# Cross-attention and FP4 feed-forward layer: attention added to x by accumulating transfers, low products of h split, block maximum of x taken a step ahead

## The chip, the cores and the metric

One core of one Trainium2 chip runs the kernel. The metric is the device time of one execution, in microseconds; the medians are over several runs. The core has four compute engines that run their own instruction streams: TensorE (PE, with weight loads shown as PEld), VectorE (DVE), ScalarE (ACT) and GpSimd (POOL). SyncE (SP) issues most of the transfers. Streams meet only at semaphores.

## What is computed

`x` is 64 x 128 x 256, the context has the same shape. The layer is

```python
q, k, v = LN(x) @ Wq + bq, ctx @ Wq + bq, ctx @ Wq + bq      # 16 wide
corr = mean over batch and channel of the circular correlation of q and k (by FFT)
w, shift = top 12 of corr, w = softmax(w)
R = sum of w * roll(v, -shift)                               # along the sequence
x = x + broadcast of R over 16 heads, reshaped @ Wout + bout
h = silu(fq(LN(x)) @ fq(w_gate).T) * (fq(LN(x)) @ fq(w_up).T)   # 704 wide
x = x + fq(h) @ fq(w_down).T
```

`fq` quantizes blocks of 16 to the FP4 grid (0, 0.5, 1, 1.5, 2, 3, 4, 6) by the scale max|block| / 6 and multiplies back. Because the heads are a broadcast reshaped along the sequence, the attention of one batch row has only 8 different rows of 256, each used by 16 positions.

## The kernel before

**Prologue (to some 122 us).** The 64 tiles of x (128 positions by 256) are loaded into `xs` and stay there. TensorE transposes x and context and projects them, the correlation is summed in one bank, the FFN weights are quantized and turned, the top 12 are found. At its end the attention (`a_sb`, 4 tiles of 128 x 257, the 257th column being minus the mean of the row) goes to `a_scratch` in DRAM from ACT's queue, one transfer for each quarter of the batch (semaphores `a_io0` to `a_io3`). `neg_mean` holds minus the mean of each row of x.

**Main loop.** 32 pairs of tiles, software-pipelined: every engine runs `for st in range(FIRST, END)`, -5 to 35, each stage working on another pair. The order of work on an engine is the order in which the code is written; an instruction behind a waiting one waits too. A pair goes through these stages:

- SP loads its attention rows (`load_attn`, L332, two transfers of 128.5 KB, each row of the scratch read by 16 partitions) two pairs ahead of their use. GpSimd adds them to `xs` (L453) and to the negative mean (L454).
- ACT squares x minus the mean with a running sum (L548, step n-3). GpSimd makes the reciprocal deviation (L428, L430, L432), ACT normalizes into `xn` (L540, one step later).
- DVE takes the maximum of each block of x (L934, `bm`), one step later the scale (L943, over h's blocks of the pair before and x's together), its reciprocal (L946) and the product `y_x` (L965). ACT's `split` (L467, L468, L470) makes an anchor and a rounded copy, DVE's `offset` (L740) and `grid` (L744) land on the FP4 grid, and L920 multiplies with the high and the low half of the scale (`sh` from ACT L557, `sl` from GpSimd L438 and L444) into fp16 `xq`. SP transposes it (L344).
- TensorE makes gate and up (L704 to L706), ACT silu (L525), DVE the product `hb` (`gate_up`, L915).
- h goes the same way: maximum L930, scale L943, product `y_h` L950, split on ACT, offset, grid, high product L920 on DVE; but its two low products are GpSimd's (`low_h`, L415, one for each tile), both at the start of a step. SP transposes both tiles (`turn_h`, L339), TensorE makes the down projection and adds x through a scaled identity (`down`, L714 to L717), ACT evacuates (`residual`, L530), SP stores (L348).

DVE's order in a step of the full loop is: gate_up of the odd tile, maximum of h, maximum of x, scale, reciprocal, y_h, x offset, x grid, two x products, y_x, gate_up of the even tile, h offset, h grid, h high product. ACT's: residual of the even tile, normalize, squares, sh, silu, residual of the odd tile, split of h, silu, split of x. GpSimd's: two low products, reciprocal deviation, L438, sl, the addition. SP's: store, two transposes of h, transpose of x, store, attention loads.

`h_c` is one buffer, so ACT's split of a pair waits until the low products of the pair before are done (`need(act, s["loh"], 2 * j)`). `xn` is one buffer too.

Of the kernel before, what the change touches and what calls it, by code (L numbers as in the profile page):

```python
# [16 lines left out]
P = 128  # L17
# [46 lines left out]
FIRST, END = -5, NP + 4  # L64
# [16 lines left out]
def build(nc, x, ctx, wq, bq, wout, bout, w_gate, w_up, w_down, out):  # L81
    es = ExitStack()
    with es:  # L83
# [66 lines left out]
        neg_mean = sb("neg_mean", [P, B])  # L150

        s_nm = sb("s_nm", [P, 2, 2])
# [5 lines left out]
        s32 = sb("s32", [P, NS])  # L158
# [5 lines left out]
        h_c = sb("h_c", [P, 2 * FF], U16)  # L164
# [4 lines left out]
        attn = w_raw[:, 2 * FF:2 * FF + 4 * DA].rearrange("p (a t n) -> p a t n", a=2, t=2)  # L169
        xn = w_raw[:, 2 * FF + 4 * DA:2 * FF + 4 * DA + 2 * D]  # L170
# [3 lines left out]
        sq_out = w_raw[:, 2 * FF + 4 * DA + 4 * D:2 * FF + 4 * DA + 6 * D].rearrange("p (t n) -> p t n", t=2)  # L174
        ctx16 = ctx_sb[:, :, :, :].rearrange("p a t d -> p (a t d)").bitcast(F16)
# [12 lines left out]
        def bank16(k):  # L188
# [4 lines left out]
            "c_loaded0", "c_loaded1", "c_loaded2", "c_loaded3", "attn_loaded0", "attn_loaded1",  # L193
# [3 lines left out]
            "x1_done", "sq_done", "pool_st", "xn_ready", "x_max", "sc_steps", "sh_done", "s32", "sl", "x_split", "x4_steps",  # L197
# [8 lines left out]
        attn_loaded = [s["attn_loaded0"], s["attn_loaded1"]]  # L206
# [10 lines left out]
        def runs_of(w, g):  # L217
            o, n = SEGS[g]
            r = RUN_H if n == FF else RUN_X
            return w[:, FF * (g % 2):FF * (g % 2) + n].rearrange("p (ih c r) -> p c ih r", ih=IH, r=r)  # L220

# [47 lines left out]
        def _(sp):  # L269
            def load_x(i):  # L270
                if i >= AHEAD:
                    sp.wait_ge(s["stats"], 2 * (i - AHEAD + 1))
                sp.dma_start(xs[:, QT * i:QT * (i + 1), :], x[QT * i:QT * (i + 1)].rearrange("b l d -> l b d")
                             ).then_inc(x_loaded[i % AHEAD], 16)
# [51 lines left out]
            def load_attn(n):  # L326
                need(sp, s["x1_done"], n - 1)
                if n % (NP // 4) == 0:
                    sp.wait_ge(a_io[n // (NP // 4)], 16)
                for t in range(2):  # L330
                    row = (2 * n + t) * ROWS8 * DA
                    sp.dma_start(attn[:, n % 2, t, :], bass.AP(a_dram.tensor, row, [[0, HEADS], [DA, ROWS8], [1, DA]])  # L332
                                 ).then_inc(attn_loaded[n % 2], 16)

# [15 lines left out]
            load_attn(0)  # L350
            load_attn(1)
# [17 lines left out]
        def _(pool):  # L369
# [18 lines left out]
            def rstd_a(i):  # L388
# [3 lines left out]
                nm = neg_mean[:, QT * i:QT * (i + 1)]  # L392
# [16 lines left out]
            def low_h(j):  # L409
                pool.wait_ge(s["h4_steps"], K_HQ * (j + 1))  # L410
                pool.wait_ge(s["sl"], j + 1 - SC0 + 1)
                for t in range(2):
                    need(pool, hT[2 * (j % 2) + t], 16 * (j // 2))
                for t in range(2):
                    pool.tensor_tensor(  # L415
                        hq[:, j % 2, t, FF:2 * FF].rearrange("p (ih r) -> p ih r", ih=IH),
                        h_c[:, :].bitcast(F16).rearrange("p (ih t r) -> p t ih r", ih=IH, t=2)[:, t],
                        sl[:, (j + 1) % 2, t * RUN_H:(t + 1) * RUN_H].unsqueeze(1).broadcast_to([P, IH, RUN_H]),
                        ALU.mult).then_inc(s["loh"], 1)

            for st in range(FIRST, END):
# [580 lines left out]
```

## Time and profile before

| what | value |
|---|---|
| median of 3 runs | 578.78 us (577.47 to 581.57) |
| profiled execution | 579.47 us, span of its instructions 577.6 us |
| busy share of the span | PE 82%, DVE 80%, ACT 68%, POOL 49% |
| granted TensorE clock, mean | 0.947 |
| main loop, 168 to 543 us | PE 345.2, DVE 345.8, ACT 290.2, POOL 218.1 us busy of 375 |

Busy time counts an instruction from its start to its end, its waits for a port included. A row of the timeline has start, duration, engine, line, operation, output and input with their shapes, and in brackets the idle time before it with what ended it. Starts of neighbouring DVE or ACT instructions can lie closer together than one of them lasts, as they overlap in the engine's pipeline; so distances are taken from start to start.

### The profile page before, as it was taken

To read this page: it belongs to the slowest core of one execution; us is meant where nothing else is said; L and a number is where in the kernel's file an instruction comes from. 1 tells how busy PE (TensorE), PEld (TensorE's weight loads), DVE (VectorE), ACT (ScalarE), POOL (GpSimd) and SP (SyncE) were. 2 spreads that over 40 slices of the span, in tenths; PEclk is the share of its full clock that TensorE was granted. 3 is DMA by queue.
4 is the path that set the end of the run, shared out by engine and by line. 5 is a ranking of instruction groups with operands and counts; after the bars stand their busy time and mean duration, and the time that the engine had idled before them with its cause. 6 is when DMAs were issued, how large, how long until landed. Compare 5 with 4: busy or idle time off the path is not lost. (4 is left out here: it accounts for less than half of the span.)

```text
span 577.6 us, 10039 instructions
## 1 busy us (share of the span) xinstructions
PE 472.7 (82%) x3454; PEld 310.6 (54%) x3454; DVE 460.9 (80%) x742; ACT 393.9 (68%) x666; POOL 281.9 (49%) x365
## 2 busy tenths in 40 slices
PE   5866677631978999999998999999989999999964
PEld 4756566420445555655555556555655556556643
DVE  3588874415698999999989999999999999998660
ACT  4425856716578887777888887878888777777530
POOL 3312353026355566666565566665655666632222
PEclk9996898875989999999999999999999999999978
DMA  8995420033145554655555556664655546544533
GB/s 283 341 350 166 146 64 2 27 92 74 37 87 123 116 119 110 124 127 115 106 120 123 119 115 116 128 124 104 113 126 124 112 108 107 109 96 90 94 77 77
DMA packets 165043, 69.19 MB, mean 120 GB/s; under 512 B 129153, under 2 KB 164737, under 8 KB 164993
## 3 DMA queue, kind: packets, MB, share of 16 engines
q1 hardware_dynamic: 164416, 68.03, 51.8%
q8 instruction: 27, 0.44, 0.3%
q10 hardware_dynamic: 576, 0.53, 0.3%
q14 instruction: 24, 0.19, 0.1%
HBM read 27.90 MB, written 9.18 MB: 64 GB/s over the span
## 5 line engine op out<-in xcount | busy, mean ns | idle before, releaser
L704 PE MATMUL ps<-guT_hi,a_xT 128*128 128x512 f16 (+1 forms) x384 | 140.4, 366 | 55.0 <-DMA a_xT<-ctx_sb 55.0
L415 POOL TENSOR_TENSOR ctx_sb<-h_c,sl 128x704 f16<-128x704 f16 x64 | 96.1, 1522 | 115.8 <-DVE ctx_sb L920 115.8
L714 PE MATMUL ps<-dT_hi,hqT 128*128 128x256 f16 x704 | 133.3, 278 | 10.7 <-DMA hqT<-ctx_sb 10.7
L705 PE MATMUL ps<-guT_lo,a_xT 128*128 128x512 f16 (+1 forms) x384 | 140.2, 365 | 0.0
L706 PE MATMUL ps<-guT_hi,a_xT 128*128 128x512 f16 (+1 forms) x384 | 140.2, 365 | 0.0
L704 PEld LDWEIGHTS ps<-guT_hi,a_xT 128*128 128x128 f16 x384 | 37.8, 98 | 103.6 <-DMA a_xT<-ctx_sb 46.0
L467 ACT ACTIVATE h_c<-y_h 128x1408 bf16<-128x1408 bf16 (+3 forms) x40 | 49.2, 1230 | 61.3 <-DVE y_h L950 36.5
L716 PE MATMUL ps<-dT_lo,hqT 128*128 128x256 f16 x384 | 90.2, 278 | 0.0
L714 PEld LDWEIGHTS ps<-dT_hi,hqT 128*128 128x128 f16 x704 | 70.1, 100 | 23.9 <-DMA hqT<-ctx_sb 11.5
L453 POOL TENSOR_TENSOR xs<-xs,w_raw 128x512 f32<-128x512 f32 x32 | 37.8, 1182 | 75.5 <-issue 49.6
L915 DVE SCALAR_TENSOR_TENSOR hb<-ps,h_in,w_raw 128x704 f32<-128x704 f32 x64 | 60.5, 945 | 4.5 <-PE ps L706 4.4
L706 PEld LDWEIGHTS ps<-guT_hi,a_xT 128*128 128x128 f16 x384 | 37.8, 98 | 39.3 <-issue 1.4
L705 PEld LDWEIGHTS ps<-guT_lo,a_xT 128*128 128x128 f16 x384 | 37.8, 99 | 38.9 <-issue 1.6
L525 ACT ACTIVATE w_raw<-ps,inv_gu 128x704 f32<-128x704 f32 x64 | 53.0, 829 | 6.0 <-PE ps L706 6.0
L740 DVE TENSOR_TENSOR h_t<-h_c,h_t 128x1408 f16<-128x1408 bf16 (+3 forms) x40 | 32.3, 808 | 27.7 <-ACT h_c L470 27.7
L557 ACT ACTIVATE sh<-bm 128x240 bf16<-128x240 f32 (+2 forms) x35 | 13.5, 385 | 59.5 <-DVE bm L943 59.5
L950 DVE TENSOR_TENSOR y_h<-hb,bm 128x1408 f32<-128x1408 f32 x32 | 52.5, 1639 | 1.1
L930 DVE TENSOR_REDUCE bm<-hb 128x88 f32<-128x1408 f32 x32 | 51.8, 1620 | 1.1
L470 ACT ACTIVATE h_c<-h_c,root 128x1408 bf16<-128x1408 bf16 (+3 forms) x40 | 52.2, 1306 | 0.0
L438 POOL TENSOR_SCALAR s<-bm 128x120 f32<-128x120 f32 (+2 forms) x35 | 48.0, 1371 | 3.7 <-DVE bm L943 1.1
L468 ACT ACTIVATE h_t<-y_h 128x1408 f16<-128x1408 bf16 (+3 forms) x40 | 48.5, 1214 | 0.0
L716 PEld LDWEIGHTS ps<-dT_lo,hqT 128*128 128x128 f16 x384 | 38.3, 100 | 8.6 <-issue 0.3
(139 smaller groups left out, 858.5 us busy)
## 6 DMA issues: line engine op xcount, KB each, us to landing
w_raw<-a_scratch SPq DMA_DIRECT2D x64, 128.5 KB, 2.6
xs<-in_x_dram SPq DMA_DIRECT2D x16, 512.0 KB, 8.7
ctx_sb<-in_ctx_dram SPq DMA_DIRECT2D x16, 512.0 KB, 7.8
out_dram<-a_xT SPq DMA_DIRECT2D x64, 128.0 KB, 2.0
hqT<-ctx_sb SPq DMA_TRANSPOSE x64, 3.7
w_raw<-in_L_ffn_w_down_dram SPq DMA_DIRECT2D x1, 704.0 KB, 9.1
w_raw<-in_L_ffn_w_gate_dram SPq DMA_DIRECT2D x1, 640.0 KB, 8.2
w_raw<-in_L_ffn_w_up_dram SPq DMA_DIRECT2D x1, 640.0 KB, 8.4
```

Source lines behind the costliest of these rows:

```text
L415: pool.tensor_tensor(hq[:, j % 2, t, FF:2 * FF].rearrange("p (ih r) -> p ih r", ih=IH), h_c[:, :].bitcast(F16).rearrange("p (ih t r) -> p ...
L467: act.activation(c.bitcast(BF16), top, ACT.Square, scale=ANCHOR_SLOPE).then_inc(done, 1)
L470: act.activation(c.bitcast(BF16), c.bitcast(BF16), ACT.Square, bias=root[:, 0:1]).then_inc(done, 1)
L525: act.activation(sil[:, i % 2, :], gu_out(i)[:, 0:FF], ACT.Silu, scale=inv_gu[:, 0:1]).then_inc(s["sil_done"], 1)
L704: pe.matmul(dst, xt[:, c, :], guT[0][:, c, n0:n1], start=(c == 0), stop=False)
L705: pe.matmul(dst, xt[:, c, :], guT[1][:, c, n0:n1], start=False, stop=False)
L706: last = pe.matmul(dst, xt[:, KC + c, :], guT[0][:, c, n0:n1], start=False, stop=(c == KC - 1))
L714: pe.matmul(dst, hqT[:, j % 4, c, :], dT_hi[:, c, :], start=(c == 0), stop=False)
L716: pe.matmul(dst, hqT[:, j % 4, c, :], dT_lo[:, c, :], start=False, stop=False)
L915: dve.scalar_tensor_tensor(out=h_v, in0=gu_out(i)[:, FF:2 * FF].rearrange(split, ih=IH), scalar=h_in[:, 0:1], in1=sil[:, i % 2, :].rearran ...
L930: dve.tensor_reduce(bm[:, 0, 0:RUN_H], hb[:, :].rearrange("p (ih b il) -> p b ih il", ih=IH, il=2), AX.XY, ALU.max, apply_absolute_value=T ...
L950: dve.tensor_tensor(y_h[:, :].rearrange(runs, ih=IH, il=2), hb[:, :].rearrange(runs, ih=IH, il=2), bm[:, 2, 0:RUN_H].unsqueeze(1).unsqueez ...
```

## The change

1. `load_attn`, `attn`, `neg_mean`, `s_nm` and the additions L453 and L454 go. `xs` gets a 257th column that holds minus the mean (written in place by GpSimd in the prologue; ACT reads it as bias). The scratch is laid out as 8 rows of all batches, and 13 transfers on GpSimd's own queue add it to `xs` while they move (`accum_op`), for 1, 2, 2, 3, then three times 3, 3, 2 pairs. The first two are issued ahead of the loop, then two in each step until all are out, each time behind the reciprocal deviation. `xs` is then loaded with rows of 1024 B at a distance of 1028 B.
2. The low products of h are issued apart: the first at the start of the step, the second at the end of GpSimd's step, behind a wait for `y_x` of the same step. `h_c` gets a second buffer; SP transposes the odd tile of h behind x.
3. The maximum of x is taken a step earlier, behind y_x and ahead of gate_up of the even tile. Normalize, reciprocal deviation and squares move a step ahead with it; `xn` gets a second buffer, and the loop starts at -4 in place of -5.
4. L438 (`s32`) goes: the factors X_SCALE and DOWN move into the constants, `bm[:, 1]` is read directly by sh and sl, and so the next scale on DVE waits for `sl` in place of `s32`.

```diff
-FIRST, END = -5, NP + 4
+FIRST, END = -4, NP + 4
+SUMS = (1, 2, 2, 3) + 3 * (3, 3, 2)
-        a_dram = nc.dram_tensor("a_scratch", [B * ROWS8, DA], F32, kind="Internal").ap()
-        xs = sb("xs", [P, B, D])
+        a_dram = nc.dram_tensor("a_scratch", [ROWS8, B * DA], F32, kind="Internal").ap()
+        xs = sb("xs", [P, B, DA])
...
-        xn = w_raw[:, 2 * FF + 4 * DA:2 * FF + 4 * DA + 2 * D]
+        xn = w_q[0][:, :].bitcast(F32)[:, 0:4 * D].rearrange("p (a n) -> p a n", a=2)
+        h_c = [h_c0[:, :], w_q[1][:, 0:2 * FF].bitcast(U16)]
...
 SP:
                 if pair_ok(st - 2):
                     turn_h(2 * st - 4)
-                    turn_h(2 * st - 3)
                 if pair_ok(st + 1):
                     turn_x(st + 1)
+                if pair_ok(st - 2):
+                    turn_h(2 * st - 3)
...
-                if pair_ok(st + 6) and st + 6 >= 2:
-                    load_attn(st + 6)
 GpSimd:
+            def add_attn(k):
+                n0 = sum(SUMS[:k])
+                if n0 % (NP // 4) == 0:
+                    pool.wait_ge(a_io[n0 // (NP // 4)], 16)
+                row, cols = 2 * n0 * DA, 2 * SUMS[k] * DA
+                pool.dma_start(xs[:, 2 * n0:2 * (n0 + SUMS[k]), :].rearrange("p t n -> p (t n)"),
+                               bass.AP(a_dram.tensor, row, [[0, HEADS], [B * DA, ROWS8], [1, cols]]), accum_op=ALU.add
+                               ).then_inc(s[f"x1_in{k}"], 16)
...
+            pool.wait_ge(s["trx"], 2 * NQ)
+            for k in range(2):
+                add_attn(k)
             for st in range(FIRST, END):
                 if pair_ok(st - 2):
-                    low_h(st - 2)
-                n = st + 3
+                    low_h(st - 2, 0)
+                n = st + 4
...
+                for k in (2 * (st - FIRST) + 2, 2 * (st - FIRST) + 3):
+                    if k < len(SUMS):
+                        add_attn(k)
                 if scaled(st):
...
-                    pool.tensor_scalar(s32[:, n0:n1], bm[:, 1, n0:n1], X_SCALE * DOWN, 1.0, ALU.mult, ALU.mult).then_inc(s["s32"], 1)
-                    pool.wait_ge(s["s32"], m + 1)
...
-                n = st + 4
-                if pair_ok(n):
...
-                    x1 = xs[:, 2 * n:2 * n + 2, :]
-                    pool.tensor_tensor(x1, x1, attn[:, n % 2, :, 0:D], ALU.add)
...
+                if pair_ok(st - 2):
+                    if pair_ok(st + 2):
+                        pool.wait_ge(s["x4_steps"], K_XQ * (st + 2) + 1)
+                    low_h(st - 2, 1)
 ACT:
-                j, n, b = st - 1, st + 2, st + 3
+                j, n, e, b = st - 1, st + 2, st + 3, st + 4
...
-                    act.wait_ge(s["x1_done"], b + 1)
+                    act.wait_ge(s[f"x1_in{sum_of(b)}"], 16)
...
-                    need(act, s["loh"], 2 * j)
+                    need(act, s["loh"], 2 * (j - 1))
 DVE:
-                if pair_ok(xb):
-                    dve.wait_ge(s["xn_ready"], xb + 1)
-                    dve.tensor_reduce(bm[:, 0, RUN_H:NS], xn.rearrange("p (b i) -> p b i", i=BLK), AX.X, ALU.max,
-                                      apply_absolute_value=True).then_inc(s["x_max"], 1)
                 if scaled(st):
...
-                    need(dve, s["s32"], m)
+                    need(dve, s["sl"], m)
...
+                if pair_ok(st + 3):
+                    dve.wait_ge(s["xn_ready"], st + 4)
+                    dve.tensor_reduce(bm[:, 0, RUN_H:NS], xn[:, (st + 3) % 2, :].rearrange("p (b i) -> p b i", i=BLK), AX.X, ALU.max,
+                                      apply_absolute_value=True).then_inc(s["x_max"], 1)
                 if tile_ok(2 * st):
                     gate_up(2 * st)
```

## Rows read from the trace of the kernel before

**Rows 1.** Timeline of DVE, one step of the loop.
```profile
168.38 1.62 DVE L950 TENSOR_TENSOR y_h<-hb,bm 128x1408 f32<-128x1408 f32 x1
169.92 0.50 DVE L740 TENSOR_TENSOR x_t<-x_c,x_t 128x512 f16<-128x512 bf16 x1
170.46 0.74 DVE L744 TENSOR_TENSOR x_c<-x_c,x_t 128x512 f16<-128x512 bf16 x1
...
174.07 0.89 DVE L740 TENSOR_TENSOR h_t<-h_c,h_t 128x1408 f16<-128x1408 bf16 x1 [0.61 <-ACT h_c L470]
...
177.71 1.62 DVE L930 TENSOR_REDUCE bm<-hb 128x88 f32<-128x1408 f32 x1
179.25 0.68 DVE L934 TENSOR_REDUCE bm<-w_raw 128x32 f32<-128x512 f32 x1
180.02 0.28 DVE L943 SCALAR_TENSOR_TENSOR bm<-bm,tiny 128x120 f32<-128x120 f32 x1
180.34 0.90 DVE L946 RECIPROCAL bm<-bm 128x120 f32<-128x120 f32 x1
181.28 1.63 DVE L950 TENSOR_TENSOR y_h<-hb,bm 128x1408 f32<-128x1408 f32 x1
```

**Rows 2.** Timeline of SP's queue and PE around the transposed x.
```profile
301.03 1.23 SPq L344 DMA_TRANSPOSE a_xT<-ctx_sb  x1
...
304.12 0.39 PE L704 MATMUL ps<-guT_hi,a_xT 128*128 128x512 f16 x1 [1.01 <-DMA a_xT<-ctx_sb]
...
307.70 0.27 PE L714 MATMUL ps<-dT_hi,hqT 128*128 128x256 f16 x1
```

**Rows 3.** Timeline of DVE in the last steps.
```profile
538.99 1.62 DVE L930 TENSOR_REDUCE bm<-hb 128x88 f32<-128x1408 f32 x1
540.65 0.64 DVE L943 SCALAR_TENSOR_TENSOR bm<-bm,tiny 128x88 f32<-128x88 f32 x1
...
542.06 1.75 DVE L950 TENSOR_TENSOR y_h<-hb,bm 128x1408 f32<-128x1408 f32 x1
```

**Rows 4.** Timeline of POOL, the step of rows 1.
```profile
176.89 3.01 POOL L415 TENSOR_TENSOR ctx_sb<-h_c,sl 128x704 f16<-128x704 f16 x2 [2.83 <-DVE ctx_sb L920]
179.98 0.19 POOL L428 TENSOR_SCALAR s_ve<-s_sq 128x2 f32<-128x2 f32 x1
...
181.32 1.73 POOL L438 TENSOR_SCALAR s<-bm 128x120 f32<-128x120 f32 x1
183.13 0.68 POOL L444 TENSOR_TENSOR sl<-s,sh 128x240 f16<-128x240 f32 x1
```

**Rows 5.** Timeline of DVE before the first h.
```profile
143.63 0.42 DVE L744 TENSOR_TENSOR x_c<-x_c,x_t 128x512 f16<-128x512 bf16 x1
```

**Rows 6.** Timeline of ACT, the step of rows 1.
```profile
178.56 0.20 ACT L548 ACTIVATION_READ_ACCUMULATOR w_raw<-xs,s_nm 128x1 f32 x1
180.34 0.40 ACT L557 ACTIVATE sh<-bm 128x240 bf16<-128x240 f32 x1 [1.59 <-DVE bm L943]
```

**Rows 7.** Timeline of POOL in the last steps.
```profile
541.80 0.52 POOL L444 TENSOR_TENSOR sl<-s,sh 128x176 f16<-128x176 f32 x1 [0.17 <-ACT sh L557]
```

**Rows 8.** The page's DMA issues: count, KB each, median us to landing.
```profile
w_raw<-a_scratch SPq DMA_DIRECT2D x64, 128.5 KB, 2.6
...
hqT<-ctx_sb SPq DMA_TRANSPOSE x64, 3.7
```

**Rows 9.** Timeline of POOL and SP's queue at the loop's start.
```profile
125.60 1.18 POOL L453 TENSOR_TENSOR xs<-xs,w_raw 128x512 f32<-128x512 f32 x1 [25.87 <-DMA w_raw<-a_scratch]
...
121.35 15.51 SPq L332 DMA_DIRECT2D w_raw<-a_scratch  x10
138.43 1.37 SPq L344 DMA_TRANSPOSE a_xT<-ctx_sb  x1
```

**Rows 10.** The page's rates in 40 slices, and all packets by size.
```profile
GB/s 283 341 350 166 146 64 2 27 92 74 37 87 123 116 119 110 124 127 115 106 120 123 119 115 116 128 124 104 113 126 124 112 108 107 109 96 90 94 77 77
DMA packets 165043, 69.19 MB, mean 120 GB/s; under 512 B 129153, under 2 KB 164737, under 8 KB 164993
```

More of the change, by code:

```diff
@@ L157, in build @@
         bm = sb("bm", [P, 3, NS])
-        s32 = sb("s32", [P, NS])
         sh = sb("sh", [P, 2, 2 * NS], BF16)
@@ L220, in runs_of, with sum_of @@
             return w[:, FF * (g % 2):FF * (g % 2) + n].rearrange("p (ih c r) -> p c ih r", ih=IH, r=r)
+        def sum_of(n):
+            return next(k for k in range(len(SUMS)) if n < sum(SUMS[:k + 1]))
         def pair_ok(n):
@@ L462, in w_hi, with split @@
                 act.activation(chunks_of(w_q[0], g), runs_of(hb, g), ACT.Copy).then_inc(s["w_hi"], 1)
-            def split(t, c, y, done, at):
+            def split(t, c, y, done, at, unit):
                 top = high_half(y).bitcast(BF16)
-                act.activation(c.bitcast(BF16), top, ACT.Square, scale=ANCHOR_SLOPE).then_inc(done, 1)
-                act.activation(t.bitcast(F16), top, ACT.Copy, scale=STICKY).then_inc(done, 1)
+                act.activation(c.bitcast(BF16), top, ACT.Square, scale=ANCHOR_SLOPE * unit).then_inc(done, 1)
+                act.activation(t.bitcast(F16), top, ACT.Copy, scale=STICKY * unit).then_inc(done, 1)
                 act.wait_ge(done, at + 1)
@@ L478, in w_split @@
                     act.wait_ge(s["root_set"], 1)
-                split(h_t[:, 0:n], h_c[:, 0:n], y_h[:, 0:n], s["w_split"], 3 * g)
+                split(h_t[:, 0:n], h_c[0][:, 0:n], y_h[:, 0:n], s["w_split"], 3 * g, 1.0)
             def evac_x(i, u):
@@ L547, in _ @@
                     for t in range(2):
-                        last = act.activation(sq_out[:, t, :], xs[:, 2 * b + t, :], ACT.Square, bias=s_nm[:, b % 2, t:t + 1],
+                        last = act.activation(sq_out[:, t, :], xs[:, 2 * b + t, 0:D], ACT.Square, bias=xs[:, 2 * b + t, D:DA],
                                               accum_out=s_sq[:, b % 2, t:t + 1])
@@ L557, in _ @@
                     act.activation(sh[:, st % 2, 2 * n0:2 * n1].rearrange("p (b two) -> p b two", two=2),
[L558 to L559 removed]
+                                   bm[:, 1, n0:n1].unsqueeze(2).broadcast_to([P, n1 - n0, 2]), ACT.Copy
+                                   ).then_inc(s["sh_done"], 1)
                 if tile_ok(2 * st):
@@ L565, in _ @@
                     act.wait_ge(s["h4_steps"], K_HQ * j + 1)
-                    need(act, s["loh"], 2 * j)
-                    split(h_t[:, :], h_c[:, :], y_h[:, :], s["h_split"], 3 * j)
+                    need(act, s["loh"], 2 * (j - 1))
+                    split(h_t[:, :], h_c[j % 2], y_h[:, :], s["h_split"], 3 * j, X_SCALE)
                 if tile_ok(2 * st + 1):
@@ L571, in _ @@
                     act.wait_ge(s["x4_steps"], K_XQ * n + 1)
-                    split(x_t[:, :], x_c[:, :], y_x, s["x_split"], 3 * n)
+                    split(x_t[:, :], x_c[:, :], y_x, s["x_split"], 3 * n, X_SCALE)
         @block.tensor
@@ L716, in down @@
                         pe.matmul(dst, hqT[:, j % 4, c, :], dT_lo[:, c, :], start=False, stop=False)
-                pe.matmul(dst, ident_out[:, :], xs[:, j, :], start=False, stop=True).then_inc(s["d_done"], 1)
+                pe.matmul(dst, ident_out[:, :], xs[:, j, 0:D], start=False, stop=True).then_inc(s["d_done"], 1)
             pe.wait_ge(s["t_steps"], 17)
@@ L972, in _ @@
                     dve.wait_ge(s["h_split"], 3 * (j + 1))
-                    offset(h_c[:, :], h_t[:, :]).then_inc(h4, 1)
+                    offset(h_c[j % 2], h_t[:, :]).then_inc(h4, 1)
                     dve.wait_ge(h4, K_HQ * j + 2)
-                    grid(h_c[:, :], h_t[:, :]).then_inc(h4, 1)
+                    grid(h_c[j % 2], h_t[:, :]).then_inc(h4, 1)
                     dve.wait_ge(h4, K_HQ * j + 3)
```

81 lines of the change are left out of this document (29 added, 52 removed).

## The prediction

> **What bounds the kernel now.** I read the engine timelines of one step of the main loop first, DVE's above all, because no engine is full over the span and the loop repeats to 0.01 us. From the y_h product at 168.38 to the next one at 181.28 is 12.90 us [rows 1]. In that step DVE waits once, 0.61 us before the h offset at 174.07, for ACT's last squaring of the anchor [rows 1]. The releases close into a ring: y_h (L950) starts ACT's split of h (L467, L468, L470); the split ends and frees offset (L740); then come grid, hi product, gate_up, the maximum of h (177.71), the maximum of x (179.25), the scale (L943, 180.02), the reciprocal (180.34), and y_h again. Start to start: y_h to offset 5.69, offset to maximum of h 3.64, maximum of h to maximum of x 1.54, to scale 0.77, to reciprocal 0.32, to y_h 0.94: 12.90. So the ring, not DVE's load, sets the step, and each thing taken out of it between 174.07 and 181.28 shortens all steps. TensorE isn't the bound: its first gate matmul waits 1.01 us (its weight load longer) for the transposed x [rows 2].
>
> **The maximum of x, one step ahead.** It leaves its place between maximum of h and scale and goes behind y_x, just ahead of gate_up, where DVE has its 0.61 us of waiting. In the ring, maximum of h to scale was 1.54 + 0.77 = 2.31; without the maximum between them it is 1.66, as the last steps show, which have no x left (538.99 to 540.65, [rows 3]). That is 0.65 a step: 12.90 to 12.25. Its 0.68 us on DVE are paid from the 0.61 of wait, and from what DVE gains below; if that cover were gone, 0.68 would be back and the gain nothing. The xn it reads is made at the start of the same ACT step, some 8 us before; the second xn buffer keeps it from a new wait.
>
> **GpSimd's part of the scales.** L438 goes (the factor moves into constants), so sl (L444) no longer stands behind it. Before, L438 started 0.04 us after y_h and took 1.74 us for 120 elements, where sl does 240 in 0.69: it stood still until y_h was through [rows 1, 4]. sl then ran at 183.13, and x offset and x grid, which start around it, took 0.50 and 0.74 (169.92 and 170.46, [rows 1]), where an undisturbed x grid takes 0.42 [rows 5]. So a DVE product with two inputs and a GpSimd product exclude each other. Where does sl now fall? Put offset at 0. ACT's squares end at 178.56 + 0.20, that is 4.69 [rows 1, 6]. GpSimd starts rstd some 0.1 later (an estimate), and its next instruction comes 181.32 - 179.98 = 1.34 after that start [rows 4]: 6.1. The scale starts at 3.64 + 1.66 = 5.30 and takes 0.28, ACT's sh follows for 0.40 [rows 6] and GpSimd answers some 0.1 to 0.2 later: 6.15. So sl runs from 6.15 to 6.84 (0.69, [rows 4]), and y_h wants to start at 6.56. In the last steps y_h started at 542.06 with sl running from 541.80 for 0.52 [rows 3, 7] and took 1.75 in place of 1.62: it was let in 0.13 us before sl's recorded end. Here that is 6.71, so 0.15 us are given back a step. Bounds: 0 (sl comes later than y_h and loses), and 0.28 (y_h waits to sl's end). I take 0.15: 12.40 a step, 0.50 saved.
>
> The Trainium skill ("SBUF — State Buffer", Who interferes with whom) says that the pair of ports is held for the full instruction and the loser fully blocks. By that rule y_h waits until 6.84, the step is 12.53 and the saving 0.37; the tail's row shows 0.13 less, and I go by the row.
>
> x offset and x grid lose their disturbance (0.07 + 0.32), which pays the rest of the moved maximum: DVE's own load is 12.90 - 0.61 - 0.39 - 0.05 = 11.85 without a wait. It stays under the ring, with 0.4 to 0.5 to spare.
>
> **The two low products of h.** Each takes 1.5 us (3.01 for two, [rows 4]). The first stays behind the hi product, under gate_up and the maximum of h, neither of which shows a disturbance. The second waits for y_x and runs under maximum of x and gate_up: 0.60 + 0.95 = 1.55 us of cover for 1.5, and the next two-input product, offset, has to wait for ACT anyway. Cost nothing; if it slips by 0.3, offset slips by less than that. In the three last steps it does give something: there the pair still ran when L943 started behind the maximum of h, and L943 took 0.64 for 88 elements in place of 0.28 for 120 or less [rows 1, 3]. 3 x 0.38 = 1.1 us.
> What comes late is the odd tile's transpose. y_h at 6.71, x offset 1.54 later, the x products 0.45 + 0.46 + 0.35 + 0.33 on to y_x at 9.84, its end 10.5, low product 10.6 to 12.1, and 3.7 us from issue to landing [rows 8]: 15.85. SP issues the x transpose first, at 9.95; TensorE starts 304.12 - 301.03 = 3.09 later, at 13.05, and reaches the down projection 307.70 - 304.12 = 3.58 after that [rows 2], at 16.6. The margin is 0.8 us, and ACT, which waits for that tile's residual, has about 1 us more. Cost nothing. On SP the store of the tile before now queues behind that transpose, some 3 us later than before; four output buffers cover it.
>
> **The accumulating transfers.** 64 loads on SP and 32 additions of 1.18 us each on GpSimd go; both are off the ring, so in the steady loop they give nothing. 13 transfers on GpSimd's queue come, two ahead of the loop, two in each step from the first, the last in the sixth step. No row shows their price. Issue on GpSimd: SP holds its queue 1.23 us for the issue of a transpose [rows 2]; bounds 0.3 to 2 us, I take 1.0. The start: the first addition began at 125.60 after waiting for its load and took 1.18, its small companion 0.20 [rows 9], so ACT could square near 127.0. Now 121.35 (the first load's issue, [rows 9]) + 1.0 + 2.6 (median landing of the plain loads, [rows 8]) = 124.95, 2.0 earlier. But the scale now waits for the sl of the step before, which stands behind two issues. Step by step (squares 1.1, rstd 1.25, normalise 1.1, maximum and scale 2) sl of the first x step ends near 136.8 and the x transpose leaves at 138.7; it left at 138.43 [rows 9]. Three issues lie on that path, so 0.5 us each gives 137.2 and 2 us each 141.7. Then the bytes: 8.4 MB in about 25 us, 340 GB/s. A plain load of 128.5 KB lands in 2.6 us, latency included. If the adding transfer moves half as fast, the first transposes of x wait behind a backlog. Bounds of the whole start: -2.5 to +12; I take +2.5, nearer the lower end as only the first two transposes meet the backlog.
> The Trainium skill ("DMA: Bandwidth & Descriptors", Anatomy of one DMA) gives about 2.0 us plus bytes at 436 GB/s for a transfer of GpSimd's queue. By it the 13 would be done as fast as they are issued and the start would cost nothing; no row shows it for an adding one.
>
> **The sum.** The first h step and 28 more have both maxima in the ring: 29 x 0.50 = 14.5. Last three: 1.1. Start: -2.5. Together 13.1 us. The profiled execution took 579.47 us with a span of 577.6, 0.7 above the median of 578.78; taken from the median: 565.7, say 566.
>
> **Rivals.** A change under 1% (5.8 us) can't be told from none here.
> 1. The race goes the other way and the start is free: 29 x 0.65 + 1.1 + 2 = 22 us: 557. For it: 6.15 against 6.56 is near; against: rstd and sh both point to sl being first. 0.10.
> 2. A new wait takes the place of the old: the odd tile's transpose lands after TensorE wants it, and the residual holds ACT's split. If low product plus transpose take 1.8 us more than worked out, the ring is 12.9 again: about 577, no change. For it: two transposes now overlap in one queue; against: the x transpose is issued 2.2 us before. 0.15 with its milder forms.
> 3. Slower: the adding transfers block the transposes. 13 x 128 rows over 16 engines are 104 pieces an engine of up to 6 KB, beside transposes of under 512 B a packet. At the plain rate of the loading phase, 350 GB/s or 22 an engine [rows 10], a piece takes 0.28 us, all 29 us; if adding doubles it, 58 us, to 180. If engines take turns packet by packet, the x transpose issued at 138.7 (129,153 small packets in 96 transposes over 16 engines are 84 an engine and transpose, [rows 10]) gets through only as this drains: up to 38 us late, a total of 600. It decides from 16 us of such delay on (a start above 15.6 + 5.8 = 21.4 us makes it slower by over 1%). For it: big against small packets; against: issue is spread over six steps. The Trainium skill ("DMA: Bandwidth & Descriptors", SWDGE vs HWDGE vs iDMA) says that each engine goes round-robin between the two kinds of queue: by that rule this rival holds in some measure. 0.10.
> 4. The forecast, with its own spread of 561 to 571: 0.65.
>
> Faster by over 1% comes from the forecast, rival 1 and nothing else: 0.75. Same 0.15, slower 0.10. The range runs from rival 1 to the mild form of rival 2: 557 to 577.
>
> **What would show it.** Step of 12.4 us between y_h rows; no wait before L740 above 0.6; L943 straight behind L930 by 1.66; x grid 0.42; y_h 1.75 to 1.8 where sl runs into it; L704's wait for the x transpose under 1.1. Wrong: a step of 12.9 with ACT waiting on d_done or TensorE on hqT (rival 2); the first x transpose leaving near 139 but TensorE starting on it after 145 (rival 3).

## The result, and the profile after

The changed kernel takes 593.94 us, median of 4 runs (591.17 to 596.08), against 578.12 us (577.37 to 581.57) for the kernel before in the same session: a ratio of 1.026, 95% interval 1.0234 to 1.0287. It is slower by 15.8 us where 12.8 us of gain were forecast. The profiled execution has a span of 594.1 us, and the mean granted clock fell from 0.947 to 0.922. One of the ten executions of e2_paced_mid below took 1689.83 us and is left out of its ratio.

The y_h rows on DVE cut both spans into three parts (first and last of their starts, before and after):

| part | before | after | difference |
|---|---|---|---|
| start to first y_h | 155.48 | 184.71 | +29.23 |
| first to last y_h | 399.09 | 385.53 | -13.56 |
| last y_h to end | 23.03 | 23.86 | +0.83 |

So loop and end gained 12.7 us of the 15.6 that were forecast for them, and the start lost twice as much. First the start. Rows of the page of the kernel after: PE's busy share and granted clock in slices of 14.85 us (TensorE stands idle in the 10th and 11th, and from the 10th to the 12th its clock is at 5 tenths), GpSimd's queue q0, and the issues with KB each and the us to landing.

```profile
PE   5767677610056999999999999999999999999865
...
PEclk9997898775558899999999999999999999999987
...
q0 software_dynamic: 1872, 8.42, 7.7%
...
xs<-a_scratch POOLq DMA_DIRECT2D x7, 771.0 KB, 18.4
xs<-a_scratch POOLq DMA_DIRECT2D x5, 514.0 KB, 7.5
```

The timeline of GpSimd, kernel after, up to the sl of the first x step; the DMA rows are issues:

```profile
121.34 2.06 POOL L402 DMA_DIRECT2D xs<-a_scratch  x2 [22.43 <-DMA a_scratch<-a_sb]
...
128.59 1.73 POOL L402 DMA_DIRECT2D xs<-a_scratch  x2
...
136.07 1.73 POOL L402 DMA_DIRECT2D xs<-a_scratch  x2
137.24 0.89 POOL L443 TENSOR_TENSOR sl<-bm,sh 128x64 f16<-128x64 f32 x1
```

By 137.8 eight of the 13 transfers are out, 19 pairs or 5.0 MB; the steps before h are only some 4 us long, so "spread over six steps" means some 20 us. Issuing costs 0.87 us each (two took 1.73). SP's queue and PE of the same kernel, around the first transposed x (the first row takes two issues together; the first of them is at 140.58):

```profile
140.58 26.66 SPq L335 DMA_TRANSPOSE a_xT<-ctx_sb  x2
```
```profile
170.69 0.59 PE L698 MATMUL ps<-guT_hi,a_xT 128*128 128x512 f16 x1 [50.08 <-DMA a_xT<-ctx_sb]
```

The transpose left at 140.58; it left at 138.43 before [rows 9]. TensorE began on it 30.1 us later. The kernel before needed 3.3 us for the same transpose:

```profile
141.74 0.58 PE L704 MATMUL ps<-guT_hi,a_xT 128*128 128x512 f16 x1 [20.99 <-DMA a_xT<-ctx_sb]
```

That accounts for the loss of the start: of its 29.2 us, 2.2 are the later issue (140.58 against 138.43), 26.8 the longer transpose (30.1 against 3.3) and 0.3 the way from TensorE's first row to the first y_h (14.0 against 13.7). DVE stood still as long, between its last x work and the first gate_up:

```profile
145.36 0.68 DVE L961 TENSOR_REDUCE bm<-w_q_hi 128x32 f32<-128x512 f32 x1
177.25 0.95 DVE L909 SCALAR_TENSOR_TENSOR hb<-ps,h_in,w_raw 128x704 f32<-128x704 f32 x1 [31.21 <-PE ps L700]
```

What the DMA engines did meanwhile is in the DMA view of four windows of the kernel after (queue and kind: packets, MB, share of 16 engines; q0 carries the additions, q1 the transposes). First 140.6 to 146:

```profile
q0 software_dynamic: 204, 1.07, 107.4%
q1 hardware_dynamic: 1, 0.00, 0.0%
```

Then the transposes alone from 146 to 150, both queues from 150 to 166, and both from 166 to 170.7:

```profile
q1 hardware_dynamic: 133, 0.03, 9.5%
```
```profile
q0 software_dynamic: 623, 3.17, 97.7%
q1 hardware_dynamic: 624, 0.16, 8.0%
```
```profile
q1 hardware_dynamic: 1260, 0.31, 89.6%
q0 software_dynamic: 68, 0.32, 33.4%
```

For over 5 us one transpose packet moved; after that 624 went for 623 rows of the additions. That is one for one: each packet of 256 B waits for a row of 5.1 KB, and the two together take 16 us x 16 engines / 624 = 0.41 us of an engine. But the turns aren't what ended the wait. A transpose of x has 1,056 packets, 66 an engine (the DMA view of e2_paced_mid has that many from 140.6 to 145.4, where the first one is issued and lands). By 166 only 1 + 133 + 624 = 758 had moved. Then the additions ran out: twelve of the 13 transfers had been issued (the 13th came at 186.33), and 68 rows were left for the last 4.7 us. At that the transposes came through at once, the first together with the second, which had been issued behind it. At 0.41 us a turn the missing 298 alone would have taken 7.6 us more, to 173.6 (an estimate from these counts). So the wait ended with the burst.

TensorE's granted clock in the two stretches without matmuls was the 1.2 GHz level, which is where the lower mean comes from; the 14.0 against 13.7 above show that it cost the start little. In the loop it was whole (windows view: duration, then busy time of PE, PEld, DVE, ACT, POOL, granted clock, DMA share, GB/s):

```profile
142.00:155.00 13.00, 0.00 (x0) 0.00 (x0) 3.35 (x8) 3.17 (x9) 3.65 (x7) 0.50 1.06 195
155.00:168.00 13.00, 0.00 (x0) 0.00 (x0) 0.00 (x0) 0.00 (x0) 0.00 (x0) 0.50 1.09 202
...
300.00:400.00 100.00, 95.05 (x593) 58.65 (x591) 94.42 (x123) 83.03 (x138) 38.09 (x48) 1.00 0.53 101
```

Now the loop. One step of DVE in the kernel after, which answers to [rows 1]:

```profile
303.03 0.89 DVE L734 TENSOR_TENSOR h_t<-w_q_lo,h_t 128x1408 f16<-128x1408 bf16 x1 [0.43 <-ACT w_q_lo L464]
...
306.67 1.62 DVE L924 TENSOR_REDUCE bm<-hb 128x88 f32<-128x1408 f32 x1
308.32 0.28 DVE L933 SCALAR_TENSOR_TENSOR bm<-bm,tiny 128x120 f32<-128x120 f32 x1
308.64 0.90 DVE L936 RECIPROCAL bm<-bm 128x120 f32<-128x120 f32 x1
309.58 1.80 DVE L940 TENSOR_TENSOR y_h<-hb,bm 128x1408 f32<-128x1408 f32 x1
...
311.75 0.43 DVE L738 TENSOR_TENSOR x_c<-x_c,x_t 128x512 f16<-128x512 bf16 x1
```

and GpSimd beside it:

```profile
309.26 0.64 POOL L443 TENSOR_TENSOR sl<-bm,sh 128x240 f16<-128x240 f32 x1 [0.23 <-issue]
```

The ring of the forecast is there. The scale starts 1.65 behind the maximum of h, x grid takes 0.43, offset waits 0.43, y_h starts inside sl and takes 1.80. That is 0.18 more than its own 1.62; read as a wait at its front, it was let in at 309.76, 0.14 before sl's recorded end at 309.90. 26 of the 31 distances between y_h rows are 12.41 to 12.43, against 12.90 before; the first is 12.78, one is 12.70, and the last three are 12.20, 12.21 and 12.67.

### The profile page after: what moved, and what is told of

The parts are those of the page before. It is cut to its first block, busy times and chain, and to the rows that moved or that the text cites. A ratio compares the mean times of both kernels' runs of the same rounds, so it can differ in the third digit from the quotient of the medians.

```text
span 594.1 us, 9852 instructions
## 1 busy us (share of the span) xinstructions
PE 472.5 (80%) x3454; PEld 308.8 (52%) x3454; DVE 455.9 (77%) x742; ACT 396.0 (67%) x666; POOL 204.7 (34%) x279
## 3 DMA queue, kind: packets, MB, share of 16 engines
q0 software_dynamic: 1872, 8.42, 7.7%
## 4 chain that ended last, share of the span: by engine, by line
DVE 44%; ACT 23%; DMA 13%; issue 9%; PE 8%; POOL 2%; SPq 1%; POOLq 0%; ACTq 0%; DVEq 0%
DVE y_h L940 9%; DVE bm L924 8%; ACT h_t L462 6%; DMA a_xT<-ctx_sb 6%; DVE hb L909 5%; DVE h_t L734 5%; DVE bm L936 5%; ACT h_c L464 4%; ACT h_c L461 4%; DMA xs<-in_x_dram 3%; ACT w_q_lo L461 3%; ACT w_q_lo L464 3%; DVE h_c L738 3%; DVE w_q_lo L738 2%; DVE bm L933 1%
## 5 line engine op out<-in xcount | busy, mean ns | idle before, releaser
L708 PE MATMUL ps<-dT_hi,hqT 128*128 128x256 f16 x704 | 132.8, 277 | 12.7 <-DMA hqT<-ctx_sb 12.7
L410 POOL TENSOR_TENSOR ctx_sb<-h_c,sl 128x704 f16<-128x704 f16 x32 | 51.5, 1610 | 107.7 <-DVE w_raw L955 52.5
L410 POOL TENSOR_TENSOR ctx_sb<-w_q_lo,sl 128x704 f16<-128x704 f16 x32 | 50.1, 1567 | 106.9 <-DVE ctx_sb L914 54.4
L708 PEld LDWEIGHTS ps<-dT_hi,hqT 128*128 128x128 f16 x704 | 69.9, 99 | 27.6 <-DMA hqT<-ctx_sb 15.5
L940 DVE TENSOR_TENSOR y_h<-hb,bm 128x1408 f32<-128x1408 f32 x32 | 57.8, 1807 | 1.1
L461 ACT ACTIVATE h_c<-y_h 128x1408 bf16<-128x1408 bf16 (+3 forms) x24 | 27.2, 1132 | 39.5 <-DVE y_h L749 23.8
L524 ACT ACTIVATE a_xT<-ps,inv_out 128x256 f32<-128x256 f32 x64 | 29.8, 465 | 20.3 <-PE ps L711 20.0
L711 PE MATMUL ps<-xs,ident_out 128*128 128x256 f32 x128 | 38.9, 386 | 0.0
L542 ACT ACTIVATE w_raw<-xs 128x256 f32<-128x256 f32 x64 | 31.7, 498 | 10.0 <-DMA xs<-a_scratch 10.0
## 6 DMA issues: line engine op xcount, KB each, us to landing
xs<-a_scratch POOLq DMA_DIRECT2D x7, 771.0 KB, 18.4
```

Of the source, the lines that this page charges most:

```text
L410: pool.tensor_tensor(hq[:, j % 2, t, FF:2 * FF].rearrange("p (ih r) -> p ih r", ih=IH), h_c[j % 2][:, :].bitcast(F16).rearrange("p (ih t r ...
L461: act.activation(c.bitcast(BF16), top, ACT.Square, scale=ANCHOR_SLOPE * unit).then_inc(done, 1)
L708: pe.matmul(dst, hqT[:, j % 4, c, :], dT_hi[:, c, :], start=(c == 0), stop=False)
L940: dve.tensor_tensor(y_h[:, :].rearrange(runs, ih=IH, il=2), hb[:, :].rearrange(runs, ih=IH, il=2), bm[:, 2, 0:RUN_H].unsqueeze(1).unsqueez ...
```

## The experiments

Two theories of the start: the additions are at fault because adding is slow (A), or any large transfer ahead of the first transpose is (B). And two of the loop: each term as forecast, or a different one that happens to have the same sum.

**e1_plain.** The same 13 transfers at the same places, as plain copies: the addition to x is left out.

```diff
-  bass.AP(a_dram.tensor, row, [[0, HEADS], [B * DA, ROWS8], [1, cols]]), accum_op=ALU.add
+  bass.AP(a_dram.tensor, row, [[0, HEADS], [B * DA, ROWS8], [1, cols]])
```

> The changed kernel with the same 13 transfers on GpSimd's queue as plain copies: the attention replaces x in place of being added (that part of the computation is left out), everything else stays. Theory A (an adding row is slow, and the engines take turns between GpSimd's transfers and the transposes, so the backlog of adding rows holds the first transposes): a plain row of 6 KB takes about 0.28 us in place of 0.5, the backlog is gone near 147 us, the first x transpose lands within 8 us of its issue, the start costs at most 5 us, total 564 to 571. Rival B (any large transfer on GpSimd's queue blocks the transposes until it is through, whatever it does): the first transpose still takes 25 us or more, total 590 or more. Step 12.42 in both.

Measured 587.32 us, ratio 1.0145 (1.0107 to 1.0183). TensorE's first row on the transposed x, and the DMA view from 150 to 160:

```profile
163.31 0.59 PE L698 MATMUL ps<-guT_hi,a_xT 128*128 128x512 f16 x1 [42.13 <-DMA a_xT<-ctx_sb]
```
```profile
q0 software_dynamic: 449, 2.21, 96.2%
q1 hardware_dynamic: 445, 0.11, 7.9%
```

The transpose was issued at 139.82, so it took 23.5 us in place of 30.1. Turn for turn again, 0.36 us a pair of packets in place of 0.41. The first y_h comes at 176.11, 8.6 us earlier than with the additions, and the whole is 6.6 us shorter. So the adding is worth only 6 to 9 us of the 29, and A falls. The expectation for B (25 us or more, 590 or more) was narrowly missed as well, but its main point stands: 23.5 of 30.1 us remain with plain transfers. Whether the transpose waits for the end of the burst or for its own turns, this run can't tell, as the copies too run out just before it lands.

**e2_paced_mid.** The additions kept, but one pair of tiles each (257 KB), three ahead of the loop and one in each step, where the two were before.

```diff
-SUMS = (1, 2, 2, 3) + 3 * (3, 3, 2)
+SUMS = 32 * (1,)
...
-            for k in range(2):
+            for k in range(3):
...
-                for k in (2 * (st - FIRST) + 2, 2 * (st - FIRST) + 3):
-                    if k < len(SUMS):
-                        add_attn(k)
+                if st + 7 < NP:
+                    add_attn(st + 7)
```

> The adding transfers stay, but one pair each, three ahead of the loop and then one a step, issued three steps before use, at their old place behind the reciprocal deviation. Theory A: no backlog when the first x transpose is issued near 138 to 140, it lands in 3 to 5 us, the start is within 2 us of the kernel before; total 561 to 566 if the step stays at 12.42. The issue of 0.9 us ahead of sl can push sl behind y_h: the step is then 12.25 and the total 556 to 560, or, if the issue itself suffers, up to 12.6. Rival B (an adding transfer is a burden wherever it stands, 8.4 MB at half speed): total 585 or more.

Measured 584.27 us, ratio 1.0079 (1.0056 to 1.0102), against 561 to 566 expected. The start is mended: the transpose leaves at 140.60, TensorE starts at 145.35, and the first y_h comes at 158.97 in place of 184.71. But a step is now 13.10 as long as transfers are issued, and 12.42 behind the last of them. DVE and then GpSimd in one such step:

```profile
302.56 2.48 DVE L939 TENSOR_TENSOR y_h<-hb,bm 128x1408 f32<-128x1408 f32 x1
```
```profile
301.98 0.89 POOL L402 DMA_DIRECT2D xs<-a_scratch  x1
302.63 0.92 POOL L442 TENSOR_TENSOR sl<-bm,sh 128x240 f16<-128x240 f32 x1
```

y_h lost 0.86 (2.48 against 1.62) to sl, though it started 0.07 before it; read as a wait at its front, it was let in at 303.42, 0.13 before sl's end. The issue pushed sl from before y_h to beside it. Two readings remain: sl had the port (D), or the issue itself held y_h (E). e6 tells them apart.

**e3_paced_end.** As e2, but issued at the end of GpSimd's step, behind the second low product.

```diff
+                if st + 7 < NP:
+                    add_attn(st + 7)
```

> As the paced kernel before it, but the issue stands at the end of GpSimd's step, behind the second low product. sl keeps its place, so the step should be 12.42 as in the changed kernel, total 561 to 566. The adding rows now run beside the transpose of the odd tile of h, 8 rows of 2 KB an engine at some 0.18 us: 1.4 us later landing, against 0.8 us of margin and 1 us of ACT's slack; if that shows, TensorE waits for hqT and the step is 12.5 to 12.9.

Measured 623.12 us, ratio 1.0769 (1.0702 to 1.0836), the slowest of all. The first y_h comes at 152.4, but steps alternate between 12.42 and 15.5 to 18.7. TensorE, then ACT, in two of the long ones:

```profile
328.88 0.39 PE L707 MATMUL ps<-dT_hi,hqT 128*128 128x256 f16 x1 [4.80 <-DMA hqT<-ctx_sb]
```
```profile
302.49 0.47 ACT L523 ACTIVATE a_xT<-ps,inv_out 128x256 f32<-128x256 f32 x1 [5.45 <-PE ps L710]
```

The issues in the DMA view of 318 to 330, with KB and median us to landing:

```profile
xs<-a_scratch POOLq DMA_DIRECT2D x1, 257.0 KB, 7.9
out_dram<-a_xT SPq DMA_DIRECT2D x2, 128.0 KB, 7.6
...
hqT<-ctx_sb SPq DMA_TRANSPOSE x2, 8.1
```

GpSimd issued its transfer at 318.97 and SP the odd tile's transpose at 319.05, the two stores right behind it. The medians are about 8 us, the transposes' in place of 3.7 [rows 8]; the one of 319.05 took 9.8, and TensorE's matmul on it is the row at 328.88. TensorE waits for hqT, ACT for TensorE's result, and the split of h stands behind ACT's residual. This is the mechanism of rival 2, with a transfer as its trigger. The expected delay of 1.4 us was far too small; why so much more came, and why only every second step was hit, stays open.

**e4_loads_mid.** No GpSimd transfers: one plain load of 257 KB a pair on SP, and GpSimd's addition (128x514) behind the first low product. All else as in the change.

```diff
-                for k in (2 * (st - FIRST) + 2, 2 * (st - FIRST) + 3):
...
+                if pair_ok(st + 5):
+                    add_attn(st + 5)
...
+                pool.tensor_tensor(x1, x1, attn[:, n % 2, :], ALU.add).then_inc(s["x1_done"], 1)
```

> No adding transfers at all: one plain load of 257 KB a pair on SP's queue, three pairs ahead, and GpSimd's addition (1.2 us) behind the first low product, everything else as changed. The start should be as before (x transpose leaves 138 to 140). The addition runs from 7.4 to 8.6 in the terms of the changed step (offset of h at 3.0), past the scale at 8.3: the scale stalls 0.2 to 0.3 us, the reciprocal deviation and sl come later, behind y_h, which then is not stalled. Step 12.4 to 12.6, total 562 to 569. If the addition costs more than that (GpSimd's chain becomes the ring), step above 12.9 and total above 577.

Measured 563.90 us, ratio 0.9734 (0.9686 to 0.9781). The transpose leaves at 138.23, TensorE starts at 141.54, the first y_h comes at 154.55, the step is 12.39. So the change without GpSimd's transfers gains 15 us, and with them it loses 16; the first y_h comes 30.2 us earlier than in the changed kernel, and the times are 30.0 apart. In the DVE row below the scale pays 0.15 for the addition that runs beside it, and y_h is free, since sl now comes after it:

```profile
301.83 0.43 DVE L940 SCALAR_TENSOR_TENSOR bm<-bm,tiny 128x120 f32<-128x120 f32 x1
...
303.23 1.62 DVE L947 TENSOR_TENSOR y_h<-hb,bm 128x1408 f32<-128x1408 f32 x1
```
```profile
300.84 1.28 POOL L413 TENSOR_TENSOR xs<-xs,w_raw 128x514 f32<-128x514 f32 x1
...
304.86 0.83 POOL L450 TENSOR_TENSOR sl<-bm,sh 128x240 f16<-128x240 f32 x1
```

**e5_short_rows.** The burst kept at its places and sizes, but cut into rows of 1 KB; what is added is x itself from the input, and the attention is left out. Against the theory that packets take turns stood another (C in the expectation), that the transpose simply waits for the bytes ahead of it.

```diff
-                pool.dma_start(xs[:, 2 * n0:2 * (n0 + SUMS[k]), :].rearrange("p t n -> p (t n)"),
-                               bass.AP(a_dram.tensor, row, [[0, HEADS], [B * DA, ROWS8], [1, cols]]), accum_op=ALU.add
+                pool.dma_start(xs[:, 2 * n0:2 * (n0 + SUMS[k]), 0:D],
+                               x[2 * n0:2 * (n0 + SUMS[k])].rearrange("b l d -> l b d"), accum_op=ALU.add
```

> The changed kernel's burst of 13 adding transfers, same bytes and same places, but cut into rows of 1 KB: what is added is x itself from the input in place of the attention, and minus the mean isn't corrected (this part of the computation is left out). Theory A (the engines take turns between GpSimd's rows and the transposes' small packets, so a transpose waits for one row per packet): a row of 1 KB takes some 0.1 us in place of 0.48, so the first x transpose, 64 packets an engine, lands 5 to 10 us after its issue in place of 28 to 30; TensorE starts before 152. Rival C (the transposes wait until the bytes that were issued before them are through): as the bytes and their rate stay, the first transpose still takes over 20 us, TensorE starts after 163.

Measured 582.63 us, ratio 1.0063 (1.0035 to 1.0090). TensorE's first row on x, the issue being at 144.99:

```profile
159.03 0.58 PE L697 MATMUL ps<-guT_hi,a_xT 128*128 128x512 f16 x1 [35.86 <-DMA a_xT<-ctx_sb]
```

The DMA view from 145 to 149.5, from 150 to 158, and from 159 to 165, when TensorE had already started:

```profile
q0 software_dynamic: 872, 0.88, 123.5%
```
```profile
q0 software_dynamic: 1149, 1.15, 94.5%
q1 hardware_dynamic: 999, 0.26, 30.3%
```
```profile
q0 software_dynamic: 795, 0.80, 89.4%
q1 hardware_dynamic: 797, 0.20, 36.4%
```

14.0 us in place of 30.1, at a rate that is no higher (144 GB/s of additions and 33 of transposes from 150 to 158, against 208 for both in the changed kernel from 150 to 166). The first transpose has landed by 159.03 while additions go on, 795 rows from 159 to 165, so it doesn't wait until the burst is through; it gets its turns. This is the only run that shows so, since in the changed kernel and in e1 the burst runs out before the turns are through. Nor does it wait for the bytes ahead of it alone, and C falls: in the changed kernel the nine transfers that were issued before the transpose or with it are 5.8 MB, GpSimd's queue had moved 6.0 MB by 158, and TensorE still waited until 170.69. The counts agree with turns. Each wait starts with a stretch in which no transpose packet moves, 5.3 us in the changed kernel (one packet before 146), 6.1 in e1 and 5.0 here; behind it are left 24.8, 17.4 and 9.1 us. 66 turns at 0.41, 0.36 and 0.13 us (8 x 16 / 999) would be 27, 24 and 9: met here, and cut short by the end of the burst in the other two. The dead time at the front is what put e5 above its expectation of 5 to 10 us; what makes it isn't shown. One doubt stays: these rows come from another place in DRAM, each read once, where the scratch's are read by 16 partitions. The issue of one such transfer cost GpSimd 1.4 us, and the transpose left at 144.99 in place of 140.58.

**e6_late_sl.** As e2, and GpSimd waits for DVE's x offset, which stands behind y_h, before sl.

```diff
+                    if pair_ok(st - 1):
+                        pool.wait_ge(s["h4_steps"], K_HQ * (st - 1) + 1)
```

> The paced kernel with one adding transfer a step ahead of sl, which took 13.10 a step as y_h grew from 1.80 to 2.48; now GpSimd waits for y_h before it makes sl. If the step was lost because sl, pushed against y_h by the issue, went first (theory D), y_h is back at 1.62 to 1.7 and the step is 12.25 to 12.4, total 558 to 564. If the descriptors that GpSimd writes for the transfer hold y_h by themselves (theory E), y_h keeps 1.9 or more and the step is 12.5 or more, total 566 or more.

Measured 564.43 us, ratio 0.9744 (0.9692 to 0.9797). DVE:

```profile
307.17 1.62 DVE L941 TENSOR_TENSOR y_h<-hb,bm 128x1408 f32<-128x1408 f32 x1
...
309.17 0.88 DVE L739 TENSOR_TENSOR x_c<-x_c,x_t 128x512 f16<-128x512 bf16 x1
```

The issue is still there, at 306.56 for 0.91, with y_h starting inside it, and y_h is whole: D holds, E falls. sl now disturbs x grid by 0.46, which isn't in the ring, and the step is 12.27 to 12.28. This is the step that the forecast's rival 1 had, at nearly its price: 12.25.

**e7_x_max_back.** e4, with the maximum of x back between maximum of h and scale.

```diff
+                if pair_ok(xb):
+                    dve.wait_ge(s["xn_ready"], xb + 1)
...
-                if pair_ok(st + 3):
-                    dve.wait_ge(s["xn_ready"], st + 4)
...
```

> The kernel with plain loads and GpSimd's addition (564 us, step 12.39), with the maximum of x back between maximum of h and scale. If the maximum in the ring is what the step gained, the step grows by 0.65 less the 0.15 by which the addition now holds up the scale, plus up to 0.15 where sl meets y_h: 12.9 to 13.05, total 578 to 583. If DVE's load and not the ring were the bound, it would stay at 12.4 to 12.5.

Measured 588.77 us, ratio 1.0167 (1.0110 to 1.0224). Apart from the first and the last three, steps are 13.08 at least, mostly 13.1 to 13.3. That is 0.69 over e4, a net of three things. From the maximum of h to the scale DVE needs 1.54 + 0.77 = 2.31 (301.18, 302.72, 303.49), in e4 1.66 (300.17 to 301.83): 0.65, as forecast. y_h has 0.18 more, and the scale, which met the addition in e4, some 0.1 less. DVE:

```profile
304.79 1.81 DVE L951 TENSOR_TENSOR y_h<-hb,bm 128x1408 f32<-128x1408 f32 x1
...
310.67 0.89 DVE L741 TENSOR_TENSOR h_t<-w_q_lo,h_t 128x1408 f16<-128x1408 bf16 x1 [1.02 <-ACT w_q_lo L471]
```

y_h lost 0.18 to sl, which makes 12.90 into 13.08. So the new way of sl without the moved maximum is a loss. The expectation (578 to 583) was missed by 6 us: 0.1 to 0.2 more in about half of the steps, and a start that is 5.4 longer than e4's (first y_h at 159.98, the transpose leaving at 141.78). The cause of neither is known.

**e8_low_together.** The changed kernel with both low products at the start of GpSimd's step.

```diff
                     low_h(st - 2, 0)
+                    low_h(st - 2, 1)
...
-                if pair_ok(st - 2):
-                    if pair_ok(st + 2):
-                        pool.wait_ge(s["x4_steps"], K_XQ * (st + 2) + 1)
-                    low_h(st - 2, 1)
```

> The changed kernel with both low products of h at the start of GpSimd's step again; only the step is read, the burst at the start stays. They end 5.9 us after the h offset, the scale wants to start at 5.3 with two inputs: it stalls by 0.4, the reciprocal deviation and sl come behind y_h. Step 12.6 to 12.75 against 12.42. If they do no harm, 12.25 to 12.42.

602.89 us, from a single execution, so only the step is read: 12.63 to 12.65 but for the first and the last four. DVE and GpSimd:

```profile
308.94 0.67 DVE L930 SCALAR_TENSOR_TENSOR bm<-bm,tiny 128x120 f32<-128x120 f32 x1
```
```profile
306.47 3.00 POOL L410 TENSOR_TENSOR ctx_sb<-w_q_lo,sl 128x704 f16<-128x704 f16 x2 [6.06 <-DVE ctx_sb L911]
```

The pair runs to 309.47, into the scale, which takes 0.67 in place of 0.28; [rows 3] have the same, 0.64, for 88 elements. Of these 0.39 us y_h gives 0.18 back, as sl now comes after it (312.21) and y_h takes 1.62: the step is 0.22 longer than with the split. So the split, which the forecast priced at nothing in the full loop, is needed to keep what the moved maximum gives: without the maximum between them, the scale comes 0.7 earlier.

**e9_both.** The additions paced (e2), sl behind y_h (e6), and the issue behind sl until the first h step.

```diff
+                if st >= 1 and st + 7 < NP:
+                    add_attn(st + 7)
...
+                    if pair_ok(st - 1):
+                        pool.wait_ge(s["h4_steps"], K_HQ * (st - 1) + 1)
...
+                if st < 1:
+                    add_attn(st + 7)
```

> The changed kernel with its adding transfers one pair each, three ahead of the loop, then one a step (behind sl until the first h step, behind the reciprocal deviation afterwards), and sl behind y_h. The step is that of the late sl, 12.27. The first scales no longer wait for an issue of 0.9 us ahead of sl, so the start should gain 1 to 3 us against the 564.4 us of the late sl: 561 to 563. If the start there came from the landing of the first adding transfer (it took some 5.7 us) and not from the issues, it stays at 564.

Measured 559.35 us, ratio 0.9669 (0.9642 to 0.9695): faster than both kernels, and 1.7 us under the lowest expected. Against e6 it is 5.1 us, of which 3.9 lie ahead of the first y_h (155.37 against 159.26). The transpose leaves at 138.80, and with transfers of 257 KB beside it TensorE starts 3.4 us later:

```profile
142.24 0.59 PE L701 MATMUL ps<-guT_hi,a_xT 128*128 128x512 f16 x1 [21.24 <-DMA a_xT<-ctx_sb]
```

Most steps are 12.26 to 12.28. The DMA rows that the changed kernel had as 13 are 32 here, with the same 8.42 MB: pacing, not volume, makes the difference. In the windows view TensorE is now busy 96.72 and DVE 97.59 of 100 us (95.05 and 94.42 in the changed kernel), so TensorE and DVE have little idle time left:

```profile
300.00:400.00 100.00, 96.72 (x605) 59.85 (x603) 97.59 (x122) 83.63 (x141) 46.14 (x59) 1.00 0.65 124
```

## Why the prediction was wrong

**The ring and the maximum of x: right.** 12.40 was forecast, 12.42 is measured. Its price of 0.65 stands in the rows of e7 against those of e4, to the hundredth. Over the 28 distances ahead of the last three the gain is 13.1 us, where 14.0 was forecast for them: the first is 12.78 and one is 12.70, while one before was 13.25.

**sl beside y_h: right, slightly low.** 0.15 was forecast, 0.18 measured, and sl did come first: 6.23 us behind the h offset (6.15 forecast), y_h 6.55. The Trainium skill ("SBUF — State Buffer", Who interferes with whom) calls the pair of ports an exclusive lock, by which y_h would wait until sl is through. By its length y_h was let in 0.14 before sl's recorded end here and 0.13 before it in e2. By that rule the step would be 12.56; the rows decide for 12.42.

**Low products and the odd tile: right.** offset never slipped, TensorE waits 0.56 for x and not for hqT, and the step agrees. e8 shows that the split had a job in the full loop too, which the forecast had only seen in the last three steps: 0.22. In the last three steps, on the other hand, 0.44 came in place of 1.1. The first two gained 0.3 each: the scale takes 0.25 in place of 0.64, and y_h 0.07 more than in [rows 3]. The last distance is 12.67, 0.16 longer than before. In it ACT's residual of a tile stands 1.61 us waiting for TensorE (until 559.53), and the split of h behind it starts 2.33 us after y_h, where it started 1.86 after it one step earlier: the mild form of rival 2, in this one step. In e6, e7 and e9 the last distance is long as well (12.6 to 12.9).

**Issue on GpSimd: right. When the transpose leaves: 1.9 us too early.** 1.0 us was taken for an issue, 0.87 is measured (bounds 0.3 to 2). 138.7 was forecast for the transpose, 140.58 is measured, inside the bounds of 137.2 to 141.7, which stood for the issue's price alone. ACT's first square started at 126.20 and not at 124.95, since the first adding transfer took 4.8 us to land, where 2.6 was taken from the plain loads [rows 8]; sl of the first x step ended at 138.13 and not at 136.8.

**The start's bytes: wrong, and this is the step that failed.** The forecast said: "Bounds of the whole start: -2.5 to +12; I take +2.5, nearer the lower end as only the first two transposes meet the backlog." Measured: +29.2, of which 26.8 are the first transpose. The number of transposes that meet the backlog doesn't matter, because the first h step can't begin before the first of them; what matters is how long that one takes. From 146 on its packets took turns with rows of 5 KB as long as there were any, and there were until TensorE was 27 us late. Rival 3 had this mechanism, that the transpose "gets through only as this drains", and its size ("up to 38 us late, a total of 600"): 27 us late and 594 came, as the additions ran dry before 170 and not at 180. Its 84 packets an engine are a mean of the short transposes of x and the longer ones of h; x has 66. It was held at 0.10 on the argument that the issue is spread over six steps, which the forecast's own text refutes: it put the 8.4 MB into about 25 us, and [rows 9] has the three x steps of the kernel before from 125.60 to 138.43, some 4 us each. The range was also cut wrongly: the upper bound of +12 and the rival's 38 spoke of the same transfer, and the range took the smaller. The sign that the forecast set for this rival, a transpose leaving near 139 and TensorE starting after 145, came true. The Trainium skill ("DMA: Bandwidth & Descriptors", SWDGE vs HWDGE vs iDMA) says that each DMA engine goes round-robin between the two kinds of queue; 623 against 624 packets agree with it to one, and so do 795 against 797 in e5. The same page's (Anatomy of one DMA) 2.0 us plus bytes at 436 GB/s gives 3.8 us for 771 KB, an estimate; the median here is 18.4 us, as its transfers queued behind one another and moved at 200 GB/s.

**The forecast's sum with the true start.** The forecast had -15.6 for loop and tail and +2.5 for the start. With +29.2 for the start it would be +13.6, or about 592; measured +15.8. All other terms together were off by 2 us (by the spans, 3: 12.7 for loop and end in place of 15.6).

## What to carry to other kernels

A transfer on one queue is not free because its engine is free: ask which small-packet transfer on another queue starts while it moves, how many packets it has on an engine, and multiply by the time of the other's row. The delay is that product or the time until the other queue runs dry, whichever is shorter. Large transfers off the critical path should be cut to what the next step needs and paced by the loop (e2, e6, e9), and kept away from the moment at which a transpose of the ring starts (e3). When a ring is shortened, look at once at what now falls beside the instructions that moved forward (here sl beside y_h, the pair of low products beside the scale): each of these took back 0.2 to 0.7 us a step, and a wait that puts the off-ring instruction second gave it back.

## What was unexpected of the hardware

- After the transpose's issue the other queue had the engines alone for 5.0 to 6.1 us (204 packets against 1 in 140.6 to 146) before the turns began. In e2, where GpSimd's queue was nearly empty, the first packet of the transpose moved 1.3 us after its issue.
- Adding transfers are only a little slower than plain ones when both take turns with transposes: 0.41 against 0.36 us a turn, 198 against 221 GB/s of their own (3.17 MB in 16 us, 2.21 in 10).
- A VectorE product that had started 0.07 us before a GpSimd product lost 0.86 us to it, where the GpSimd one stood directly behind a transfer's issue (e2). What its recorded start leaves out isn't shown; the same issue without sl behind it cost y_h nothing (e6).
- One adding transfer of 257 KB a step, issued near the odd tile's transpose, cost several us in every second step (e3): a collision at the wrong moment is dearer than its bytes.
